# Hybrid block: one block-diagonal product inside the state chain, ScalarE evictions with scalings, output projection over two heads, a redrawn plan

## The chip, the cores and the metric

The kernel runs on one core of one Trainium2 chip. The metric is the device time of one execution in microseconds. Five instruction streams run in their own order: TensorE (PE), VectorE (DVE), ScalarE (ACT), GpSimd (POOL) and SyncE (SP), which issues the DMAs. They meet only at semaphores.

## The reference

The input x is 2 sequences of 1024 tokens with 256 features, in float32. Three layers are applied, each added to x:

1. A gated delta-rule attention with 16 heads of 128 features. From the normed input come q, k and v (projection, causal convolution over 4 tokens, silu; q and k scaled to length 1), a decay g per feature and a factor beta per token. Then per head, token by token:

```python
S = S * gt[..., None]
pred = jnp.einsum('bhk,bhkv->bhv', kt, S)
delta = (vt - pred) * bt[..., None]
S = S + kt[..., None] * delta[:, :, None, :]
o = jnp.einsum('bhk,bhkv->bhv', qt, S)
```

   o is normed, multiplied by a sigmoid gate and projected back to 256 features by Wo.
2. A gated FFN of width 1024, a state-space scan (512 channels, 16 states), and the same FFN again.

## The kernel before

**Attention phase.** The 1024 tokens are cut into 2 segments (`NSEG`) of 512, and a unit of work g is one head in one segment, for both sequences: 32 units (`NG`), called heads below. In a unit the tokens of each sequence form 8 chunks of 64 (`NC`, `CH`), and a tile of 128 partitions holds one chunk of both sequences. Inside a chunk the delta rule is a triangular system. Its inverse is built for 32-token blocks in `inverse`, from products that `products` makes in five levels, and the two 32-blocks of a chunk are then joined in `Y64`.

Before the change the system is solved ahead of the chain: `solved` multiplies the inverse with all values (U, L522) and with all keys (W, L531), for which `turn_k` turns the decayed keys (L498). ScalarE copies these results out of PSUM (L1015, L1027, L1036). The chain `state` then has two steps for each of the 8 chunks: TensorE makes pred (L567) and the state's part of the output (L572), VectorE subtracts pred (L827); TensorE makes the outer product (L577), VectorE forms the new state with the chunk's decay (L832). After every fourth chunk come the products within the chunks (L583). `output` norms, gates and turns the result, projects it with Wo (L609, four products a head), and VectorE adds each into x (L870).

**What sets the order.** Every engine's program is made by `att_drive`: each stage of each head is a generator, and `braid` runs its steps in the order of keys 100·(g+lag)+place, with lag and places from `PLACES`. One head is thus 100 units of place. The same keys rule on all five engines, so each engine has one fixed order. `EARLY_AT`, `FRONT_AT` and `FFN_AT` do the same for the first two FFN tiles and for the phase behind attention. Weights come by SyncE, one head ahead.

**Tail phase.** After a barrier (`all_over`) come the scans of 4 units, the rest of the FFN tiles, and the stores. The change touches only the places there.

## Time and profile before

| what | value |
|---|---|
| median of three runs (lowest, highest) | 2775.3 us (2770.25, 2782.81) |
| the profiled execution, its time | 2776.06 us |
| the profiled execution, its span | 2774.3 us |
| PE busy | 2495.6 us, 90% of the span, 46512 matmul records |
| DVE busy | 2124.1 us, 77% |
| ACT busy | 1393.4 us, 50% |
| POOL busy | 1260.3 us, 45% |

The span is the time from the first to the last instruction of the profiled execution; 1.8 us of its own time lie around it. One float32 product of the program appears as two matmul records, a transpose as one. Busy time counts overlapping instructions once. The attention phase takes the first 2001 us of the span, the tail the rest.

### The profile page before, as it was taken

The page shows a single profiled execution, that of the slowest core. Times are in us where ns is not written, and L with a number is a line of the kernel's source. Part 1 is how long each engine was busy: PE and PEld are TensorE (multiplying, and loading weights), DVE is VectorE, ACT ScalarE, POOL GpSimd, SP SyncE. Part 2 cuts the span into 40 slices and gives each one's busy share as a digit, 9 for nine tenths or more (in the row PEclk, how much of TensorE's full clock was granted, in tenths as well). Part 3 has the DMA queues.
Part 4 walks back from the last instruction along what each step waited for, and adds up shares of the span by engine and source line. Part 5 has one row for each costly group of instructions (what it writes and reads, how often), then busy time and mean ns, then how long its engine had stood idle before and what let it go on. Part 6 is the DMA issues. An engine that isn't in the chain of part 4 may idle for free.

```text
span 2774.3 us, 102732 instructions
## 1 busy us (share of the span) xinstructions
PE 2495.6 (90%) x46512; PEld 1483.1 (53%) x46512; DVE 2124.1 (77%) x3249; ACT 1393.4 (50%) x2647; POOL 1260.3 (45%) x989
## 2 busy tenths in 40 slices
PE   6799999999999999999999999989878889888888
PEld 3466666666666566666666666664323333333333
DVE  3778888888888787888888877863229989999981
ACT  3445555455545455455555554533255645556342
POOL 0545545555555444555555454540014645546540
PEclk9899999999999999999999999999989999999999
DMA  1000000000000000000000000010012323323320
GB/s 52 22 12 14 13 20 13 15 13 20 13 16 13 13 20 13 16 13 20 13 15 15 18 13 15 7 52 1 25 38 92 126 92 112 112 90 127 121 95 15
DMA packets 52069, 105.61 MB, mean 38 GB/s; under 512 B 7084, under 2 KB 11948, under 8 KB 51376
## 3 DMA queue, kind: packets, MB, share of 16 engines
q1 hardware_dynamic: 51632, 99.04, 11.0%
q8 instruction: 365, 5.98, 0.9%
q14 instruction: 72, 0.59, 0.1%
HBM read 96.65 MB, written 2.37 MB: 36 GB/s over the span
## 4 chain that ended last, share of the span: by engine, by line
PE 60%; DVE 15%; issue 12%; ACT 11%; POOL 1%; DMA 1%; SPq 0%; DVEq 0%; ACTq 0%; POOLq 0%
PE bank L359 8%; PE bank L461 5%; DVE hs L1683 5%; PE bank L609 4%; PE bank L424 4%; PE pair L577 3%; PE bank L1500 3%; PE pair L567 3%; PE bank L393 2%; PE bank L583 2%; PE bank L549 2%; PE bank L531 2%; PE bank L1422 2%; PE bank L572 2%; DVE cv L651 2%
## 5 line engine op out<-in xcount | busy, mean ns | idle before, releaser
L1989 POOL TENSOR_TENSOR dBu<-dtu,Bn 128x1024 f32<-128x1024 f32 x128 | 306.2, 2394 | 232.1 <-DVE hc L1690 231.8
L651 DVE SCALAR_TENSOR_TENSOR cv<-raw,taps,cv 128x1024 f32<-128x1024 f32 x288 | 385.1, 1338 | 16.4 <-ACT cv L917 14.0
L359 PE MATMUL bank<-xn,W 128*128 128x512 f32 x768 | 381.9, 621 | 0.0
L1176 POOL TENSOR_TENSOR kL<-kL,tot 128x512 f32<-128x512 f32 x128 | 195.2, 1525 | 258.0 <-PE bank L424 258.0
L916 ACT ACTIVATE raw<-bank 128x512 f32<-128x512 f32 x192 | 114.9, 599 | 370.9 <-PE bank L359 370.1
L1500 PE MATMUL bank<-hc,eye 128*128 128x512 f32 x512 | 249.1, 615 | 56.2 <-DVE hc L1690 56.1
L1887 ACT ACTIVATE bank<-dtv,m_A 128x512 f32<-128x512 f32 x256 | 174.3, 687 | 209.6 <-DVE hs L1683 208.8
L1151 POOL TENSOR_TENSOR R<-qn,gate 128x1024 f32<-128x1024 f32 x32 | 108.6, 3393 | 269.5 <-ACT gate L977 269.5
L1500 PEld LDWEIGHTS bank<-hc,eye 128*128 128x128 f32 x512 | 93.7, 193 | 201.8 <-DVE hc L1690 110.6
L359 PEld LDWEIGHTS bank<-xn,W 128*128 128x128 f32 x768 | 132.3, 191 | 112.9 <-issue 103.0
L1690 DVE TENSOR_TENSOR hc<-hs,Cn 128x1024 f32<-128x1024 f32 x128 | 171.9, 1343 | 11.5 <-PE bank L1500 7.3
L1178 POOL TENSOR_TENSOR R<-R,tot 128x512 f32<-128x512 f32 x128 | 168.4, 1316 | 0.0
L1683 DVE TENSOR_TENSOR_SCAN hs<-bank,carry,dBu 128x512 f32<-128x512 f32 x128 | 158.8, 1270 | 1.5 <-ACT bank L1887 1.5
L1683 DVE TENSOR_TENSOR_SCAN hs<-bank,dBu 128x512 f32<-128x512 f32 x128 | 150.8, 1206 | 10.1 <-POOL dBu L1989 5.0
L737 DVE TENSOR_TENSOR R<-R,tot 128x512 f32<-128x512 f32 x128 | 111.5, 871 | 47.0 <-PE bank L424 47.0
L424 PE MATMUL bank<-R,kL 128*32 128x64 f32 (+1 forms) x10240 | 135.3, 205 | 9.9 <-POOL R L1151 9.0
L577 PE MATMUL pair<-vT,kT 64*128 64x128 f32 x1024 | 129.9, 331 | 14.2 <-DVE vT L827 13.4
L424 PEld LDWEIGHTS bank<-R,kL 128*32 128x32 f32 x10240 | 115.5, 111 | 47.1 <-issue 37.3
L1073 ACT ACTIVATE cen<-bank 128x128 f32<-128x128 f32 x256 | 67.4, 278 | 145.4 <-PE bank L583 145.4
L461 PE MATMUL bank<-XY,Bc 32*32 32x32 f32 x8192 | 101.0, 195 | 42.1 <-issue 34.5
L827 DVE TENSOR_TENSOR vT<-vT,pair 128x128 f32<-128x128 f32 x256 | 71.5, 279 | 86.5 <-PE pair L567 86.2
L609 PE MATMUL bank<-WT,WO 128*128 128x512 f32 x256 | 137.1, 618 | 0.3 <-ACT WT L1090 0.3
(267 smaller groups left out, 5657.4 us busy)
## 6 DMA issues: line engine op xcount, KB each, us to landing
Bn<-ssm_rows SPq DMA_DIRECT2D x128, 256.0 KB, 3.5
Cn<-ssm_rows SPq DMA_DIRECT2D x128, 256.0 KB, 3.2
W<-in_head_w SPq DMA_DIRECT2D x32, 448.0 KB, 3.3
WO<-in_out_w SPq DMA_DIRECT2D x32, 192.0 KB, 2.3
xT<-in_xT SPq DMA_DIRECT2D x1, 2048.0 KB, 8.1
out_xT<-xT SPq DMA_DIRECT2D x4, 512.0 KB, 3.8
xn<-in_w_gate SPq DMA_DIRECT2D x1, 1024.0 KB, 5.8
xn<-in_w_up SPq DMA_DIRECT2D x1, 1024.0 KB, 8.3
```

Of the source, the lines that this page charges most:

```text
L359: m = pe.matmul(psum[bank][:, :], w[:, (kind * KT + k) * P:(kind * KT + k + 1) * P], xn[:, k, b, cols], start=k == 0, stop=k == KT - 1)
L424: m = pe.matmul(o, block(kL[s], c, b, u), r)
L461: m = pe.matmul(psum[INV][quad(w), c * SUBB:(c + 1) * SUBB], lhsT[quad(w), c, :], rhs[quad(w), c, :])
L577: m = pe.matmul(psum[CHAIN[b]][:, P:2 * P], kT[s][rows_of(b), c, :], vT[g % 3][rows_of(b), c, :])
L609: pe.matmul(psum[bank][:, :], WO[s][:, (k + 1) * P:(k + 2) * P], WT[s][:, 4 * hh:4 * hh + 4, :].rearrange("p c n -> p (c n)")).then_inc(wo ...
L651: dve.scalar_tensor_tensor(cv[m % 2][:, :, :], raw[m % 2][:, :, i:i + SEG], taps[:, h, KQV[n], i:i + 1], cv[m % 2][:, :, :], MUL, ADD).the ...
L1176: pool.tensor_tensor(Lv[:, :, 0, :], Lv[:, :, 0, :], spread(two[:, :, 1], 2, half), MUL).then_inc(up_l.sem)
L1500: m = pe.matmul(psum[Y_BANKS[jj]][:, :], eye[:, :], hc[(u * PAIRS + p) % BACK][:, jj, :], start=False, stop=p % HALF_P == HALF_P - 1, skip ...
L1683: dve.tensor_tensor_scan(hs[p % BACK][:, jj, :], psum[A_BANKS[at % NA]][:, :], dBu[p % AHEAD][:, jj, :], carry[:, b, i:i + 1] if seg else ...
L1690: dve.tensor_tensor(hc[p % BACK][:, :, :], hs[p % BACK][:, :, :], spread(Cn[p % DEEP][:, :], 1, DT2), MUL).then_inc(hc_set.sem)
L1887: act.activation(psum[A_BANKS[at % NA]][:, :], dtv[u % 2][:, j, :], ACT.Exp, scale=m_A[:, j, n:n + 1]).then_inc(dA_set.sem)
L1989: pool.tensor_tensor(dBu[at % AHEAD][:, :, :], dtu[s][:, half * DT2:(half + 1) * DT2, :], spread(Bn[at % DEEP][:, :], 1, DT2), MUL).then_i ...
```

## The change

- The chain has three steps for each chunk. pred is made from the decayed keys as they are (`R`). VectorE forms r = v·|k| − pred in one instruction. TensorE multiplies r with `Y64`, which is now a full 128 by 128 block-diagonal matrix for both sequences. ScalarE evicts the result with the scale beta/|k|² (`bs`), which gives the delta. The outer product follows as before, and VectorE only adds it, since ScalarE has scaled the old state by the chunk's decay.
- `solved`, the turning of the decayed keys, and their five kinds of evictions are gone; so are GpSimd's `side` and its making of `Y64`.
- The evictions of the turned v and the turned k and of AT's upper part move from VectorE to ScalarE, and four copies for `Y64` come onto ScalarE.
- Wo's product runs for every second head: two heads are accumulated in one PSUM bank, and VectorE adds it into x half as often.
- `qn` and `gate` have one buffer in place of two, `WO` and `bs` three in place of two; `th` and `ogT` get their own. ScalarE now waits with the gate's first eviction for the first level of the head before.
- All places are new. The columns of `PLACES` are, in order: conv 0, 1, 2, dots, gating, turn_v, products, inverse, turn_k, (solved, gone), out_gate, state, output.

```diff
@@ PLACES @@
-    (0, [-8.2, 14.4, 26.7, 27.6, 33.5, 34.5]),
...
-    (2, [7.5, 13.7, 17.5, 19.7, 23.3, 28, 31.9, 35.9, 37.3, 47.4, 50.9, 53.2, 55.5, 57.8, 67, 69.4, 72.9,
-         73.7]),
...
+    (0, [-9.7, -9.7, -3.8, 0.5, 15.2, 39.7]),
+    (0, [46.8, 46.9, 47.1, 58.2, 74.2, 106.2]),
+    (0, [-3.5, 0.5, 0.5, 54.8, 72.5, 76.3]),
+    (1, [-20.5, -10.7, -7.1, -5.5, 3.6, 5.3, 19.2, 30.6, 36.5, 41.8, 48.9, 55.6, 59.8, 65.8, 79]),
+    (1, [10, 21.7, 23.9, 31.1, 36.6, 48.2, 48.2, 53.5, 53.5, 59.3, 59.9, 62.5, 64.6, 64.7, 65.8, 71.4, 76.1,
+         83.3, 89.2, 93.2, 95.4]),
+    (1, [80.2, 82.1]),
+    (2, [18.1, 32.8]),
+    (2, [-4.3, 0.9, 6.3, 13.8, 18.9, 21.3, 24.2, 31.2, 31.3, 33.9, 36.6, 37.6, 39.9, 47.1, 48.8, 51.7, 54.9,
+         59.2, 59.4, 61.5, 63.3, 67.9, 70.5, 72.3, 75.7, 79.4]),
...
@@ hybrid_block @@
-        Y64 = sa("Y64", [P, NC, 2, SUBB])
+        Y64 = [sa(f"Y64_{i}", [P, NC, P]) for i in range(2)]
...
@@ att_tensor @@
-            def solved(g):
-                for q in range(2):
-                    bank = take()
-                    if q == 0:
-                        pe.wait_ge(*off_kept.at(g))
-                        pe.wait_ge(*vT_set.at(g, 1))
-                    for c in range(4 * q, 4 * q + 4):
-                        for b in range(NB):
-                            m = pe.matmul(psum[bank][rows_of(b), (c % 4) * P:(c % 4 + 1) * P],
-                                          Y64[rows_of(b), c, :, :].rearrange("p h i -> p (h i)"), vT[g % 3][rows_of(b), c, :])
-                    m.then_inc(u_full.sem)
-                    held[bank] = u_set.at(g, q)
-                    yield
-                w_banks = [take() for b in range(NB)]
-                pe.wait_ge(*kRT_set.at(g, 1))
-                for c in range(NC):
-                    for b in range(NB):
-                        m = pe.matmul(psum[w_banks[b]][:, c * CH:(c + 1) * CH], kRT(g)[rows_of(b), c, :],
-                                      Y64[rows_of(b), c, :, :].rearrange("p h i -> p (h i)"))
-                m.then_inc(w_full.sem)
-                for b in range(NB):
-                    held[w_banks[b]] = wT_set.at(g, b)
...
                     if c:
                         pe.wait_ge(*s_set.at(g, c - 1))
                     else:
-                        pe.wait_ge(*wT_set.at(g, 1))
+                        pe.wait_ge(*up_k.at(g, NL))
                         if g == 0:
                             pe.wait_ge(*s_zeroed.at(0))
                     for b in range(NB):
-                        m = pe.matmul(psum[CHAIN[0]][rows_of(b), 0:P], WT[s][:, c, rows_of(b)], src[:, b, :])
+                        m = pe.matmul(psum[CHAIN[0]][rows_of(b), 0:P], R[s][:, 0, c, b, :], src[:, b, :])
                     m.then_inc(pred_full.sem)
+                    yield
+                    pe.wait_ge(*r_set.at(g, c))
+                    pe.matmul(psum[CHAIN[1]][:, 0:P], Y64[s][:, c, :], vT[g % 3][:, c, :]).then_inc(solved.sem)
                     if c == 4:
                         pe.wait_ge(*og_set.at(g, 0))
+                    elif c == 0:
+                        pe.wait_ge(*up_q.at(g))
+                        if g:
+                            pe.wait_ge(*og_set.at(g - 1, 1))
                     for b in range(NB):
                         pe.matmul(psum[OUT][rows_of(b), (c % 4) * P:(c % 4 + 1) * P], R[s][:, 1, c, b, :], src[:, b, :],
                                   start=c % 4 == 0, stop=False, skip_group_check=True)
                     yield
                     pe.wait_ge(*d_set.at(g, c))
+                    if c == 0:
+                        pe.wait_ge(*kT_set.at(g, 1))
+                        if g:
+                            pe.wait_ge(*s_set.at(g - 1, NC - 1))
                     for b in range(NB):
                         m = pe.matmul(psum[CHAIN[b]][:, P:2 * P], kT[s][rows_of(b), c, :], vT[g % 3][rows_of(b), c, :])
                     m.then_inc(outer_full.sem)
                     yield
                     if c % 4 == 3:
+                        if c == 3:
+                            pe.wait_ge(*at_set.at(g))
                         for c4 in range(c - 3, c + 1):
                             for b in range(NB):
                                 m = pe.matmul(psum[OUT][rows_of(b), (c4 % 4) * P:(c4 % 4 + 1) * P],
...
                 for hh in range(2):
                     for k in range(KT):
-                        bank = take()
-                        if k == 0:
-                            pe.wait_ge(*ogT_set.at(g, hh))
-                        pe.matmul(psum[bank][:, :], WO[s][:, (k + 1) * P:(k + 2) * P],
-                                  WT[s][:, 4 * hh:4 * hh + 4, :].rearrange("p c n -> p (c n)")).then_inc(wo_full.sem)
-                        held[bank] = x_added.at(g, 2 * hh + k)
+                        if g % 2:
+                            bank = take()
+                            if k == 0:
+                                pe.wait_ge(*ogT_set.at(g, hh))
+                                if hh == 0:
+                                    pe.wait_ge(*wo_scaled.at(g))
+                            for i in range(2):
+                                m = pe.matmul(psum[bank][:, :], WO[(g - 1 + i) % 3][:, (k + 1) * P:(k + 2) * P],
+                                              ogT[i][:, 4 * hh:4 * hh + 4, :].rearrange("p c n -> p (c n)"),
+                                              start=i == 0, stop=i == 1)
+                            m.then_inc(wo_full.sem)
+                            held[bank] = x_added.at(g // 2, 2 * hh + k)
                         if 2 * hh + k < 3:
...
@@ att_vector @@
-                dve.wait_ge(*at_diag.at(g))
-                for w in (0, 2):
-                    m = dve.tensor_tensor(AT[s][quad(w), :, SUBB:CH], view[quad(w), :, 1, :],
-                                          spread(bs[s][quad(w), :], 2, SUBB), MUL)
-                m.then_inc(at_set.sem)
...
                 for c in range(NC):
-                    src = S[:, h, :, :] if c % 2 == 0 else Sx[:, :, :]
                     dst = Sx[:, :, :] if c % 2 == 0 else S[:, h, :, :]
                     dve.wait_ge(*pred_full.at(g, c))
                     if c == 0:
-                        dve.wait_ge(*u_set.at(g, 1))
-                    dve.tensor_tensor(vT[g % 3][:, c, :], vT[g % 3][:, c, :], psum[CHAIN[0]][:, 0:P],
-                                      SUB).then_inc(d_set.sem)
-                    yield
+                        dve.wait_ge(*vT_set.at(g, 1))
+                        dve.wait_ge(*k_norm.at(g))
+                        dve.wait_ge(*off_kept.at(g))
+                    dve.scalar_tensor_tensor(vT[g % 3][:, c, :], vT[g % 3][:, c, :], knorm[g % 3][:, c:c + 1],
+                                             psum[CHAIN[0]][:, 0:P], MUL, SUB).then_inc(r_set.sem)
+                    yield
+                    yield
+                    dve.wait_ge(*s_scaled.at(g, c))
                     dve.wait_ge(*outer_full.at(g, c))
-                    for b in range(NB):
-                        m = dve.scalar_tensor_tensor(dst[:, b, :], src[:, b, :], tot_chunk[s][:, c, b:b + 1],
-                                                     outer[:, b, :], MUL, ADD)
-                    m.then_inc(s_set.sem)
+                    dve.tensor_tensor(dst[:, :, :], dst[:, :, :], outer, ADD).then_inc(s_set.sem)
                     yield
                     if c == 3:
...
@@ att_scalar @@
-                    if b == 0 and g >= 2:
-                        act.wait_ge(*w_full.at(g - 2))
-                    act.activation(by_batch(gate[s])[:, b, :, :], psum[bank][:, :].rearrange("p (c t) -> p c t", t=CH),
+                    if b == 0 and g:
+                        act.wait_ge(*level.at(g - 1, 1))
+                    act.activation(by_batch(gate)[:, b, :, :], psum[bank][:, :].rearrange("p (c t) -> p c t", t=CH),
...
+                for half in range(2):
+                    bank = turn.next()
+                    act.wait_ge(*v_turned.at(g, half))
+                    if g >= 3:
+                        act.wait_ge(*within_full.at(g - 3, 1))
+                    act.activation(vT[g % 3][:, 4 * half:4 * half + 4, :].rearrange("p c d -> p (c d)"), psum[bank][:, :],
+                                   ACT.Copy).then_inc(vT_set.sem)
+                    if half == 0:
+                        yield
...
+                act.wait_ge(*bo_set.at(g))
+                act.wait_ge(*at_diag.at(g))
+                for w in (0, 2):
+                    m = act.activation(AT[g % 2][quad(w), :, SUBB:CH],
+                                       psum[PROD][quad(w), :].rearrange("p (c a i) -> p c a i", c=NC, a=2)[:, :, 1, :],
+                                       ACT.Copy)
+                m.then_inc(at_set.sem)
...
+                act.wait_ge(*y_set.at(g, NL - 1))
+                if g >= 2:
+                    act.wait_ge(*solved.at(g - 2, NC - 1))
+                else:
+                    act.wait_ge(*y64_zeroed.at(g))
+                for w in range(4):
+                    m = act.activation(Y64[g % 2][quad(w), :, quad(w)], XY[quad(w), 1, :, :], ACT.Copy)
+                m.then_inc(y64_set.sem)
...
+                    act.wait_ge(*k_turned.at(g, q))
+                    if g >= 2:
+                        act.wait_ge(*outer_full.at(g - 2, NC - 1))
+                    act.activation(kT[s][:, 4 * q:4 * q + 4, :].rearrange("p c d -> p (c d)"), psum[bank][:, :],
+                                   ACT.Copy).then_inc(kT_set.sem)
+                    if q == 0:
...
+                h, s = g % H, g % 2
+                for c in range(NC):
+                    src = S[:, h, :, :] if c % 2 == 0 else Sx[:, :, :]
+                    dst = Sx[:, :, :] if c % 2 == 0 else S[:, h, :, :]
+                    if c:
+                        act.wait_ge(*s_set.at(g, c - 1))
+                    else:
+                        act.wait_ge(*up_t.at(g, NL - 1))
+                        act.wait_ge(*(s_set.at(g - 1, NC - 1) if g else s_zeroed.at(0)))
+                    for b in range(NB):
+                        m = act.activation(dst[:, b, :], src[:, b, :], ACT.Copy, scale=tot_chunk[s][:, c, b:b + 1])
+                    m.then_inc(s_scaled.sem)
+                    yield
+                    if c == 0:
+                        act.wait_ge(*bs_set.at(g))
+                    act.wait_ge(*solved.at(g, c))
+                    act.activation(vT[g % 3][:, c, :], psum[CHAIN[1]][:, 0:P], ACT.Copy,
+                                   scale=bs[g % 3][:, c:c + 1]).then_inc(d_set.sem)
+                    yield
+                    yield
+                    if c == 3:
+                        yield
 
...
```

## Rows read from the trace of the kernel before

**Rows 1.** Busy time by stretch: columns are stretch, length, PE, PEld, DVE, ACT, POOL, granted clock, DMA.

```profile
1142.00:1579.00 437.00, 412.75 (x11169) 280.01 (x11168) 364.43 (x664) 240.91 (x504) 234.57 (x192) 1.00 0.05 16
229.96:288.40 58.44, 53.99 (x1398) 36.84 (x1400) 46.34 (x84) 30.30 (x64) 29.05 (x28) 0.94 0.05 14
171.00:1695.00 1524.00, 1429.79 (x37712) 968.24 (x37712) 1244.95 (x2243) 816.97 (x1706) 778.93 (x688) 0.98 0.05 15
1695.00:2001.00 306.00, 279.68 (x4880) 171.99 (x4878) 168.30 (x317) 123.91 (x256) 85.16 (x73) 0.96 0.05 16
2101.00:2693.00 592.00, 518.51 (x1142) 212.06 (x1140) 554.14 (x491) 309.58 (x480) 314.93 (x146) 0.98 0.34 110
```

**Rows 2.** Waits of PE from 1142 to 1579 us: total us, times, longest.

```profile
PE bank L461 <- issue: 12.4, 13, 1.4
PE bank L449 <- issue: 5.2, 4, 1.5
PE pair L577 <- DVE vT L827: 1.6, 2, 0.8
```

**Rows 3.** Groups by form on PE, 1142 to 1579 us: count | busy us, mean ns | idle before.

```profile
L609 PE MATMUL bank<-WT,WO 128*128 128x512 f32 x64 | 34.4, 619 | 0.0
L549 PE MATMUL bank<-WO,hga 128*128 128x128 f32 x128 | 18.8, 289 | 0.2 <-issue 0.2
L522 PE MATMUL bank<-vT,Y 64*64 64x128 f32 x256 | 17.5, 275 | 0.5
L531 PE MATMUL bank<-Y,gate 64*128 64x64 f32 x256 | 16.0, 275 | 0.0
L567 PE MATMUL pair<-S,WT 128*64 128x128 f32 x128 | 14.1, 297 | 0.7 <-issue 0.6
L498 PE MATMUL bank<-eye,R 128*128 128x128 f32 x64 | 10.0, 279 | 0.0
```

**Rows 4.** Groups by form on VectorE, 1142 to 1579 us.

```profile
L651 DVE SCALAR_TENSOR_TENSOR cv<-raw,taps,cv 128x1024 f32<-128x1024 f32 x72 | 94.3, 1309 | 0.6
L870 DVE TENSOR_TENSOR xT<-xT,bank 128x512 f32<-128x512 f32 x32 | 21.9, 684 | 9.4 <-PE bank L609 9.4
L832 DVE SCALAR_TENSOR_TENSOR Sx<-S,tot_chunk,pair 128x128 f32<-128x128 f32 x64 | 18.9, 336 | 0.0
L827 DVE TENSOR_TENSOR vT<-vT,pair 128x128 f32<-128x128 f32 x64 | 17.9, 280 | 13.5 <-PE pair L567 13.4
L747 DVE TENSOR_TENSOR Bc<-bank,bm 128x256 f32<-128x256 f32 x40 | 16.5, 413 | 0.0
L699 DVE TENSOR_TENSOR vT<-bank,knorm 128x512 f32<-128x512 f32 x16 | 11.0, 686 | 5.3 <-PE bank L405 5.3
```

**Rows 5.** Groups by form on ScalarE, 1142 to 1579 us.

```profile
L917 ACT ACTIVATE cv<-bank,taps 128x512 f32<-128x512 f32 x48 | 32.8, 683 | 0.0
L1073 ACT ACTIVATE cen<-bank 128x128 f32<-128x128 f32 x64 | 16.9, 278 | 26.2 <-PE bank L583 26.2
L1053 ACT ACT_TABLE_LOAD x8 | 10.3, 1283 | 0.1
L1036 ACT ACTIVATE WT<-bank 128x512 f32<-128x512 f32 x16 | 8.7, 595 | 17.6 <-PE bank L531 17.6
L1001 ACT ACTIVATE Z<-bank 32x256 f32<-32x256 f32 x16 | 6.0, 378 | 0.3
L1056 ACT ACTIVATE WO<-WO,norm_w 128x256 f32<-128x256 f32 x8 | 4.0, 497 | 0.0
```

**Rows 6.** Timeline: start us, us, instruction [idle before]; one chunk's steps, at two places.

```profile
1254.84 0.44 PE L567 MATMUL pair<-Sx,WT 128*64 128x128 f32 x4
...
1255.33 0.29 DVE L827 TENSOR_TENSOR vT<-vT,pair 128x128 f32<-128x128 f32 x1 [0.50 <-PE pair L567]
...
1844.15 0.28 DVE L827 TENSOR_TENSOR vT<-vT,pair 128x128 f32<-128x128 f32 x1
...
1844.49 0.49 PE L577 MATMUL pair<-vT,kT 64*128 64x128 f32 x4 [0.39 <-DVE vT L827]
```

251 lines of the change are left out of this document (91 added, 160 removed), and 12 rows, old and new, of tables (EARLY_AT, PLACES).

## The prediction, made before the run

> **What bounds the kernel now.** I read the busy time by stretch first. From 1142 to 1579 us eight heads pass, at full clock: 437.0 / 8 = 54.6 us a head, of which TensorE is busy 412.75 / 8 = 51.6 us, VectorE 45.6, ScalarE 30.1, GpSimd 29.3 [rows 1]. So TensorE idles 3.0 us a head. The waits say what for: nearly all of it is "issue" in front of streams of tiny products (12.4 and 5.2 us in eight heads at L461 and L449), where no engine is waited for; the chain (L577 behind L827) costs 1.6 us in eight heads, 0.2 a head [rows 2]. The attention phase is therefore bound by TensorE's own work, and the order written into the places hides every other engine. The granted clock adds to it: over 27 heads from 171 to 1695 us it is 0.98, and a head takes 1524 / 27 = 56.4 us; in one head at 0.94 it is 58.4 us [rows 1]. The tail is another matter: from 2101 to 2693 us VectorE is busy 554 of 592 us [rows 1], and the change alters only places there.
>
> **TensorE's work.** Removed in each head: U, 17.5 / 8 = 2.19 us; W, 16.0 / 8 = 2.00; the turning of the decayed keys, 10.0 / 8 = 1.25 [rows 3]. Together 5.44 us. Added: eight products of 128 by 128 with 128 columns, 16 records. The nearest row is the gate product L549, of just this shape: 18.8 / 128 = 0.147 us a record, so 16 × 0.147 = 2.35 us [rows 3]. Bounds: the narrower L567 has 14.1 / 128 = 0.110, so 1.76 us; a product that stands alone shows its first record's 289 ns and then 0.147, so 8 × 0.436 = 3.5 us. I take 2.35, since other products stand around most of them. pred from `R` has the shape of the pred from WT, so its cost stays. Wo's product keeps its count: four products a head before, eight for every second head after, so nothing is saved on TensorE. Net 5.44 − 2.35 = −3.1 us a head. Records fall from 1396 to 1396 − 72 + 16 = 1340 a head (11169 / 8, rows 1), and the issue stalls, which stand before streams of tiny products, I let fall by the same 4%: −0.1 us.
>
> **VectorE's work.** Gone: two evictions of the turned v at 0.686 [rows 4], two of the turned k of the same size, two of AT's upper part (a bank read of 256 columns, as L747, 0.41), and two of the four additions into x at 0.684: 1.37 + 1.37 + 0.82 + 1.37 = 4.9 us. In the chain a chunk had 0.280 + 2 × 0.336 = 0.95 us [rows 4]; now it has one three-operand instruction of 128 columns, priced as L832, 0.336, and one addition of 256 columns, as L747, 0.413: 0.75, so −1.6 us in eight chunks. VectorE goes from 45.6 to about 39 us. It is not the bound, so this is worth nothing by itself; it makes the answers in the chain earlier.
>
> **ScalarE's work.** Removed: six evictions of 512 columns at about 0.60 = −3.6 us. Added: four of these for turned v and k, 2.4; AT and the four copies into `Y64`, 6 × 0.378 = 2.3 (L1001) [rows 5]; eight evictions of the solved chunk, 128 columns from PSUM as L1073, 0.278, with a scale vector, which from L1036 to L917 costs 0.683 − 0.595 = 0.09: 8 × 0.37 = 2.9; sixteen scalings of the state, 128 columns within SBUF. L1056 has 256 columns with a scale in 0.497; by L1073 and L1001 a column costs (378 − 278) / 128 = 0.8 ns, so 0.39 us each, 6.3 us (bounds 0.28 and 0.50 each: 4.5 and 8.0). Sum +10.3 us: ScalarE goes to some 40 us, 77% of a head of 52. Its cover is that TensorE still has more; it becomes a server that every chunk needs, in a fixed order with other work.
>
> A rule of the Trainium skill speaks against this move: "ScalarE: Activation LUTs", Rules for kernel authors, says to do plain multiplications and additions on VectorE and budgets about 0.3 us and 0.83 ns an element for each ScalarE instruction, 0.41 us for 128 columns. By it the 24 new small instructions take 9.8 us, where my terms say 9.2; the trace agrees with its slope and shows less fixed cost, and the sum stays. What it would mean if ScalarE came to be waited for is the slower rival.
>
> **GpSimd and SyncE.** GpSimd loses the side product and `Y64`; it has half its time free, so zero. SyncE's loads only change the buffer they go to; the third `WO` buffer lets Wo stay until the second head of a pair has used it. Zero.
>
> **The chain.** Each chunk has three round trips where it had two. From row to row: pred starts at 1254.84 and VectorE at 1255.33, 0.49 later; VectorE ends at 1844.43 and TensorE starts at 1844.49, 0.06 later [rows 6]. Between pred and the solving product lie 0.49 + 0.34 + 0.06 = 0.89 us; between that and the outer product about 0.29 + 0.05 + 0.37 + 0.06 = 0.77; from there to the next pred 0.49 + 0.05 + 0.41 + 0.06 = 1.0. TensorE must have other work for it. I merged the new places as `braid` does and priced what stands between. After pred: 0.55 us or more in every chunk (an inverse step of 0.69, the dots, the gate product), with pred's own 0.3 just enough. After the outer product: 0.55 to 1.1 us beside its own 0.42, enough within 0.1. After the solving product: itself and the state's part of the output, 0.29 + 0.32 = 0.61, and a block of 0.69 or so in chunks 0, 1, 4, 5 and 6; in chunks 2, 3 and 7 nothing, 0.15 us short each. That makes 0.6 us a head if VectorE and ScalarE are free when asked. They are not always: a convolution step holds VectorE 1.31 us [rows 4], a table load ScalarE 1.28 [rows 5]. The second half of the new chain (places 47 to 76) has no projection beside it; about 14 us of VectorE's work stand against 13 of TensorE's there. I add 0.6 for this, 1.2 against 0.2 now, so +0.9 to 1.0 us a head. Behind a waiting product stands all of TensorE's order, so each such wait counts in full. Low end: 0; high end in the rival.
>
> **Single buffers.** The gate's first eviction now waits for level one of the head before, whose VectorE part is some 4 us after the first level's products. ScalarE stands in that wait, with the chain's first delta behind it. In the merged order the projections are ahead of it; I count it within the 1.2.
>
> **The sum.** A head: 54.6 − 3.1 − 0.1 + 0.9 = 52.3 us, −2.3 us. I apply it to 32 heads, the last ones included (from 1695 to 2001 us TensorE is still busy 280 of 306 us, rows 1): −74 us. When the last head runs out, its longer chain has only the early FFN beside it: +2. The tail's new places: 0, between −8 and +8, as VectorE leaves only 38 us of 592 unused there [rows 1]. The profiled execution, 2776.06 us, becomes 2704; it stands 0.8 above the median of the runs, so 2703.
>
> **Rivals.**
> (a) *The order hides everything.* Waits stay at 0.2: −3.2 us a head, −102: about 2674. For it: today's order hides two round trips almost wholly. Against: three chunks have no block between solving and outer product.
> (b) *A third round trip that is half covered.* 2.4 us of waits a head: −1.0 × 32 = −32: about 2743. For it: the stretch without projections and ScalarE at 77%.
> (c) *ScalarE's order sets the pace; slower than before.* The eight deltas queue on ScalarE behind silus, exps and table loads of about 1.1 to 1.3 us, three loads a head [rows 5]. It decides from 3.2 + 0.2 = 3.4 us of waits a head, 0.43 a chunk. If each chunk lost 0.8 us, 6.4 a head: +6.2 − 3.2 = +3.0 × 32 = +96: about 2871; at 0.5 a chunk 2794. Against: ScalarE has 12 us a head free, and its copies of Z, also in a chain, cost TensorE nothing today [rows 2].
> (d) *The clock.* If all heads ran at 54.6's clock, 27 × 1.8 = 49 us would be won; if all ran as the one at 0.94, 27 × 2.0 = 54 lost [rows 1]. Nothing in the change pushes it clearly; it widens the range.
> (e) *No gain, since what is removed was cover.* U, W and the turns give the other engines 5 us a head to catch up, and without them the waits grow by as much: about 2775. Against: three of these blocks lie at the seam between heads, where TensorE waits for nobody.
>
> **Chances.** Forecast (2680 to 2725) 0.50; (a) 0.13; (b), to 2761, 0.21; (e) 0.05; (c) 0.11. About 0.5%, 14 us, is what a measurement of this kernel can tell from no change: faster 0.84, same 0.05, slower 0.11. The range 2657 to 2766 takes in (a) with some luck of the clock, and (b).
>
> **What would show it.** In the changed profile, in a stretch at full clock: a head of 52 to 52.5 us; TensorE busy 48.5; the new product at 0.15 us a record; ScalarE near 40 us busy, VectorE 39; new lines in TensorE's waits, 1 us a head for VectorE's r and ScalarE's delta, most of it at chunks 2, 3 and 7. It is wrong if TensorE's waits for ScalarE pass 2 us a head (b, c), if the clock in the heads leaves 0.96 to 1.0, or if the tail moves by more than 8 us.

## The result and the profile after

| | before | after |
|---|---|---|
| median of four runs each (lowest, highest) | 2775.69 us (2770.25, 2782.81) | 2854.74 us (2848.57, 2860.58) |
| ratio, 95% interval | | 1.0283 (1.025 to 1.0316) |
| span of the profiled execution | 2774.3 us | 2855.4 us |

The change makes the kernel 2.8% slower; 2703 us had been forecast, and 2766 was the end of the range. The two spans differ by 81.1 us. SyncE's loads of `W` mark the heads: from the sixth to the last lie 26 heads in both kernels. They took 1464.97 us before and 1540.82 after, +76. What comes ahead of them is 9 us shorter, from the last load to the attention's end there are 337 us in place of 306 [rows 1], +31, and the tail is 16 us shorter.

Busy time by stretch, columns as in [rows 1]. First the 26 heads of the kernel before:

```profile
229.96:1694.93 1464.97, 1375.67 (x36314) 931.31 (x36316) 1198.47 (x2160) 786.70 (x1643) 749.89 (x661) 0.98 0.05 15
```

The kernel after: its 26 heads, an odd head at full clock, one at 0.92, an even head, the end of the attention.

```profile
220.60:1761.42 1540.82, 1387.57 (x34858) 922.62 (x34860) 1164.47 (x1743) 1079.87 (x2422) 682.46 (x610) 0.94 0.05 14
570.56:629.45 58.89, 54.03 (x1350) 34.96 (x1352) 45.01 (x70) 41.31 (x93) 26.08 (x25) 1.00 0.05 14
1287.89:1351.17 63.28, 57.37 (x1350) 37.57 (x1352) 47.42 (x70) 41.63 (x93) 26.05 (x22) 0.92 0.04 13
1351.17:1405.61 54.44, 47.48 (x1334) 31.84 (x1336) 44.72 (x65) 41.43 (x93) 26.40 (x22) 1.00 0.05 15
1761.42:2098.00 336.58, 296.78 (x5032) 175.39 (x5032) 167.81 (x267) 175.78 (x392) 83.89 (x69) 0.93 0.04 15
```

Per head (divide by 26): the period goes from 56.35 to 59.26 us. TensorE is busy 53.37 us where it was 52.91, and idle 5.89 where it was 3.43. The clock is 0.94 against 0.98. ScalarE is at 41.5 us (forecast 40), VectorE at 44.8 (forecast 39), GpSimd at 26.2.

Waits of TensorE in the 26 heads after (as [rows 2]):

```profile
PE bank L458 <- issue: 54.5, 44, 2.3
PE bank L372 <- issue: 33.9, 26, 2.5
PE bank L458 <- ACT Z L969: 23.2, 24, 1.0
PE pair L531 <- DVE Sx L791: 13.7, 13, 1.3
PE bank L420 <- DVE Ac L696: 6.4, 23, 0.3
PE pair L535 <- DVE vT L785: 4.1, 6, 0.7
PE pair L552 <- ACT vT L1047: 3.2, 6, 0.6
```

The reader is to see which rows are short: the two that the new round trip brought, `L535` for VectorE's r and `L552` for ScalarE's delta, have 7.3 us in 26 heads, 0.3 a head. What grew is "issue", from 2.8 to 3.5 us a head (the largest row before is the one below), and waits that the prediction did not have at all: 0.9 us a head for ScalarE's `Z` and 0.5 for the state.

```profile
PE bank L461 <- issue: 47.7, 38, 2.7
```

The solving product on TensorE after, 163 to 1761 us (27 heads; as [rows 3]):

```profile
L535 PE MATMUL pair<-vT,Y 128*128 128x128 f32 x432 | 106.3, 330 | 6.8 <-DVE vT L785 4.1 <-issue 2.7
```

The solving product takes 106.3 / 27 = 3.9 us a head by its own rows at the clock of the run, 0.25 a record, where 0.147 had been taken.

**Where the clock goes.** TensorE, kernel after, at the start of an odd head: products, the table load that stands ahead of `Z` on ScalarE, then the same time by stretches of 5 us.

```profile
1172.15 0.67 PE L458 MATMUL bank<-Z,XY 32*32 32x32 f32 x54
1174.20 0.31 PE L458 MATMUL bank<-Z,XY 32*32 32x32 f32 x10 [1.38 <-issue]
...
1178.04 0.44 PE L372 MATMUL bank<-qn 128*32 128x32 f32 x15 [1.48 <-issue]
1178.41 0.80 PE L535 MATMUL pair<-vT,Y 128*128 128x128 f32 x2
...
1188.94 0.75 PE L458 MATMUL bank<-Z,XY 32*32 32x32 f32 x64 [0.96 <-ACT Z L969]
...
1185.90 1.28 ACT L900 ACT_TABLE_LOAD   x1
```

```profile
1170.00:1175.00 5.00, 3.62 (x191) 2.80 (x184) 2.73 (x5) 4.95 (x9) 2.61 (x2) 0.98 0.27 95
1175.00:1180.00 5.00, 3.52 (x150) 2.82 (x148) 2.80 (x6) 3.31 (x5) 1.07 (x1) 0.50 0.03 7
1180.00:1185.00 5.00, 5.00 (x169) 4.15 (x160) 1.79 (x4) 1.08 (x3) 1.49 (x2) 0.50 0.02 5
1185.00:1190.00 5.00, 4.03 (x153) 2.98 (x148) 4.16 (x8) 4.35 (x11) 0.76 (x2) 1.00 0.01 3
```

Two stalls of 1.4 us stand 2.4 us apart in a long run of tiny products. In the stretch with the first of them TensorE is busy 3.62 of 5 us, and by its end the clock falls from full (2.4 GHz) to half (1.2 GHz), for about 10 us. A solving product then takes 0.80 us where it takes 0.49. The even head from 1351 us has stalls of 1.45 and 1.33 us, 2.1 us apart, and keeps the full clock:

```profile
1356.00:1361.00 5.00, 2.61 (x168) 2.13 (x167) 2.50 (x4) 4.05 (x6) 1.45 (x2) 1.00 0.01 3
```

So the clock falls behind such stalls in some places and not in others; what decides it is not shown. The Trainium skill, "TensorE: Matmul & The Clock Gate", section "HAM oscillation — how this bites in real kernels", tells of longer gaps, waits for transfers between bursts of products: the clock falls in the gap and the next burst starts slow. The slow products behind the stalls of the odd head agree; the even head has no such fall.

**VectorE and GpSimd on one port.** Timeline of the kernel after:

```profile
1371.62 3.35 DVE L691 TENSOR_TENSOR R<-kL,gate 128x1024 f32<-128x1024 f32 x1
...
1371.52 2.36 POOL L1145 TENSOR_TENSOR R<-qn,gate 128x1024 f32<-128x1024 f32 x1 [6.67 <-PE bank L560]
```

The same pair in the kernel before:

```profile
1267.73 1.23 DVE L713 TENSOR_TENSOR R<-kL,gate 128x1024 f32<-128x1024 f32 x1 [1.38 <-ACT gate L977]
...
1267.78 3.40 POOL L1151 TENSOR_TENSOR R<-qn,gate 128x1024 f32<-128x1024 f32 x1 [7.82 <-ACT gate L977]
```

VectorE's instruction is called rk below. Both multiply two tensors in SBUF. The one that starts first, by 0.05 or 0.10 us, takes its own time, and the other takes that and its own: 1.2 + 2.2 = 3.4, 2.3 + 1.1 = 3.4. The order has turned round: before, GpSimd, which has time, paid; after, VectorE pays. The Trainium skill, "SBUF — State Buffer", section "Who interferes with whom", states that a VectorE instruction with two inputs in SBUF contends with a GpSimd instruction that reads SBUF, and that the order of issue decides who blocks. The rows agree.

The same happens to an instruction of 8 columns, `osum`, which took 0.16 us in the kernel before (L852) and now starts while GpSimd makes its masks:

```profile
1375.49 2.14 DVE L809 SCALAR_TENSOR_TENSOR osum<-norms,osum 128x8 f32<-128x8 f32 x1
...
1373.85 3.75 POOL L1151 TENSOR_TENSOR bm<-masks,bs 128x1536 f32<-128x1536 f32 x1
```

It ends when they are done, and its mean over the 26 heads is 2.02 us. In the whole run ScalarE waits 50 us for it. This was not tested by a run.

### The profile page after: what moved, and what is told of

The parts are those of the page before. It is cut to its first block, busy times and chain, and to the rows that moved or that the text cites. A ratio compares the mean times of both kernels' runs of the same rounds, so it can differ in the third digit from the quotient of the medians.

```text
span 2855.4 us, 100153 instructions
## 1 busy us (share of the span) xinstructions
PE 2512.6 (88%) x44720; PEld 1470.2 (51%) x44720; DVE 2071.2 (73%) x2737; ACT 1759.9 (62%) x3610; POOL 1184.8 (41%) x927
## 4 chain that ended last, share of the span: by engine, by line
PE 59%; DVE 16%; issue 13%; ACT 11%; DMA 1%; POOL 0%; DVEq 0%; SPq 0%; ACTq 0%; POOLq 0%
PE bank L354 7%; PE bank L458 6%; DVE hs L1663 5%; PE bank L590 4%; PE pair L552 4%; PE bank L1480 3%; PE pair L535 3%; PE bank L420 3%; PE pair L531 3%; PE bank L513 3%; PE bank L1402 2%; PE bank L543 2%; PE bank L372 2%; PE bank L446 2%; ACT vT L1047 1%
## 5 line engine op out<-in xcount | busy, mean ns | idle before, releaser
L634 DVE SCALAR_TENSOR_TENSOR cv<-raw,taps,cv 128x1024 f32<-128x1024 f32 x288 | 393.0, 1365 | 35.3 <-ACT cv L875 34.6
L1166 POOL TENSOR_TENSOR kL<-kL,tot 128x512 f32<-128x512 f32 x128 | 211.6, 1653 | 426.6 <-PE bank L420 425.9
L354 PE MATMUL bank<-xn,W 128*128 128x512 f32 x768 | 360.7, 610 | 0.0
L1480 PE MATMUL bank<-hc,eye 128*128 128x512 f32 x512 | 254.6, 626 | 47.6 <-DVE hc L1670 47.5
L354 PEld LDWEIGHTS bank<-xn,W 128*128 128x128 f32 x768 | 141.0, 193 | 151.8 <-issue 147.9
L1047 ACT ACTIVATE vT<-pair,bs 128x128 f32<-128x128 f32 x256 | 93.9, 367 | 161.4 <-PE pair L535 161.3
L458 PE MATMUL bank<-Z,XY 32*32 32x32 f32 x8192 | 109.7, 200 | 74.7 <-issue 46.1
L785 DVE SCALAR_TENSOR_TENSOR vT<-vT,knorm,pair 128x128 f32<-128x128 f32 x256 | 86.5, 338 | 111.8 <-PE pair L531 99.2
L1145 POOL TENSOR_TENSOR R<-qn,gate 128x1024 f32<-128x1024 f32 x32 | 78.2, 2444 | 208.2 <-PE bank L560 196.0
L715 DVE TENSOR_TENSOR R<-R,tot 128x512 f32<-128x512 f32 x128 | 123.4, 964 | 52.2 <-PE bank L420 52.2
L552 PE MATMUL pair<-vT,kT 64*128 64x128 f32 x1024 | 135.4, 343 | 14.5 <-ACT vT L1047 5.1
L458 PEld LDWEIGHTS bank<-Z,XY 32*32 32x32 f32 x8192 | 91.0, 111 | 106.7 <-issue 60.0
```

The costliest lines, as they stand in the source:

```text
L354: m = pe.matmul(psum[bank][:, :], w[:, (kind * KT + k) * P:(kind * KT + k + 1) * P], xn[:, k, b, cols], start=k == 0, stop=k == KT - 1)
L458: m = pe.matmul(psum[INV][quad(w), c * SUBB:(c + 1) * SUBB], lhsT[quad(w), c, :], rhs[quad(w), c, :])
L552: m = pe.matmul(psum[CHAIN[b]][:, P:2 * P], kT[s][rows_of(b), c, :], vT[g % 3][rows_of(b), c, :])
L634: dve.scalar_tensor_tensor(cv[m % 2][:, :, :], raw[m % 2][:, :, i:i + SEG], taps[:, h, KQV[n], i:i + 1], cv[m % 2][:, :, :], MUL, ADD).the ...
L1166: pool.tensor_tensor(Lv[:, :, 0, :], Lv[:, :, 0, :], spread(two[:, :, 1], 2, half), MUL).then_inc(up_l.sem)
L1480: m = pe.matmul(psum[Y_BANKS[jj]][:, :], eye[:, :], hc[(u * PAIRS + p) % BACK][:, jj, :], start=False, stop=p % HALF_P == HALF_P - 1, skip ...
```

## The experiments

"Waits", "period" and "idle" are those of the same 26 heads. Each group of runs shared its runs of the kernel before; the ratio is to those.

**The tail alone.** The kernel before with the four lists of places of the tail from the change:

```
-FFN_FROM = [0, 0, 52.3, 142.6, 242.7, 342.7, 430.8, 531.5]
+FFN_FROM = [0, 0, 52.3, 142.5, 242.6, 334.2, 426.8, 526.6]
...
```

> The kernel before with only the places of the tail phase (scans and late FFN) taken from the change. The tail took 773 us before (2001 to 2774) and 757 in the changed kernel (2098 to 2855). Theory: the redrawn tail places are worth this by themselves: about -16 us, 2760 us, the attention phase unchanged at 2001 us. Rival: the shorter tail is what the longer attention phase left behind or chance, and here it is within 5 us of before.

Measured: 2759.65 us (2754.39 to 2764.14), ratio 0.9946 (0.9929 to 0.9963). The tail's new places give 15 us by themselves, and this is the fastest kernel here that computes the whole: it beats both.

**One more product in each chunk, or eight in a row.** In the kernel before:

```
                     m.then_inc(pred_full.sem)
+                    pe.matmul(psum[CHAIN[1]][:, 0:P], eye[:, :], eye[:, :])
```

> The kernel before with one more 128x128x128 product in each chunk of the chain (identity by identity, into an unused part of a bank, never read), put between pred and the state's part of the output; no wait is added. Theory A (a short product that stands alone between others of another shape costs TensorE 0.42 us and makes its neighbours dearer by 0.1 to 0.15, as L535 in the changed kernel shows): +4.0 to 4.6 us a head, +130 to +145 us, about 2910. Rival (the price of my prediction, 0.29 us each, 2.35 us a head): +75 us, 2850.

```
+                        for c in range(NC):
+                            pe.matmul(psum[CHAIN[1]][:, 0:P], eye[:, :], eye[:, :])
                     for c in range(4 * hh, 4 * hh + 4):
```

> The same eight extra products a head, but in a row in front of the gate products, which have the same shape. Both theories: 0.147 us a record, 2.35 us a head, +75 us, 2850. By theory A this is 50 to 70 us faster than the run with them inside the chain; by the rival the two are equal within 10 us.

Measured: 2860.4 us, ratio 1.0302 (1.0272 to 1.0332), for the scattered ones: +85.6 us, 2.68 a head over all 32, 0.33 a product. In a row: 2827.28, ratio 1.0189 (1.0156 to 1.0221): +52 us, 1.64 a head, 0.205 a product. The 26 heads of the two runs:

```profile
230.85:1770.28 1539.43, 1485.76 (x36730) 987.51 (x36732) 1188.68 (x2159) 783.79 (x1643) 714.78 (x660) 0.98 0.05 14
232.20:1750.35 1518.15, 1427.36 (x36730) 981.16 (x36732) 1203.85 (x2160) 786.55 (x1643) 740.44 (x661) 0.98 0.05 15
```

By these periods a product costs 0.36 us scattered and 0.26 in a row. So a product of this shape alone between others costs 1.4 to 1.6 times what it costs in a row. The first expectation was too high by 50 us. In a row the added 2.0 us of busy time lengthen the period by all of it, 2.05; the scattered ones add 4.2 us of busy time and 2.9 to the period, since they take up 1.4 us of what had been waits. The mean clock is 0.98 in both runs, as in the kernel before.

**Places set by hand.** The changed kernel with the shared stages at their places of before and places that I set for the chain:

> The changed kernel with other places for the heads: those of the kernel before for all stages it shares, and the chain's 26 steps set by hand so that a block of other work stands between nearly all of them. Theory B (the redrawn order leaves TensorE waiting; 2.4 us a head more idle time than before): idle falls by 2 us a head, about 2790 us. Rival (the third round trip and ScalarE's load make the waits in any order, and the clock falls with them): within 15 us of the changed kernel, 2840 to 2870.

Measured: 3201.15 us, ratio 1.1533 (1.1496 to 1.157). TensorE waited 89 us for `cen`, 85 for the delta, 69 for r. Nothing follows on the change, but much on the order: places alone moved this kernel by 346 us.

**The gating behind k's step.**

```
-    (0, [56.8, 59.4, 65.1, 74.8]),
-    (0, [-3.5, 0.5, 0.5, 54.8, 72.5, 76.3]),
+    (0, [56.8, 59.4, 66.2, 74.8]),
+    (0, [-3.5, 0.5, 0.5, 66.5, 72.5, 76.3]),
```

> The changed kernel with two places redrawn: the gating step (exp, ln) is put behind the dots' step in the order, so that both exps and the ln of a head stand together and the silu of k goes before them. Table loads fall from 5 to 3 a head. Theory (the loads are one of the uncounted costs: 2.6 us of ScalarE a head, in front of Z, for which TensorE waits 0.9 us a head at L458): that wait falls to under 0.3 and the head by 0.8 to 1.0 us, 30 us in all, about 2825. Rival (the loads lie in ScalarE's free time, and Z is late for other reasons): less than 5 us, and within 2850 to 2858.

Measured: 2954.7 us, ratio 1.0637 (1.0619 to 1.0655). The loads fell to three, and the wait for `Z` went from the list. But its longest wait is now

```profile
PE pair L552 <- ACT vT L1047: 103.5, 32, 3.6
```

once in each head. ScalarE and TensorE there:

```profile
1440.59 1.04 ACT L932 ACTIVATE sq<-sq 128x1024 f32<-128x1024 f32 x1
1441.66 1.15 ACT L934 ACTIVATE sq<-sq,biases 128x1024 f32<-128x1024 f32 x1
1442.72 0.58 ACT L946 ACTIVATE vT<-bank 128x512 f32<-128x512 f32 x1
1443.19 0.68 ACT L1041 ACTIVATE S<-Sx,tot_chunk 128x128 f32<-128x128 f32 x2
1443.78 0.35 ACT L1047 ACTIVATE vT<-pair,bs 128x128 f32<-128x128 f32 x1
...
1439.81 0.49 PE L535 MATMUL pair<-vT,Y 128*128 128x128 f32 x2
...
1444.18 0.80 PE L552 MATMUL pair<-vT,kT 64*128 64x128 f32 x4 [3.52 <-ACT vT L1047]
```

The solved chunk was ready at 1440.3, and three small steps behind a table load and four long ones stood ahead of its delta. My repair removed two table loads a head, 2.6 us of ScalarE's work, and put a wait of 3.2 us into every head: this is rival (c), made by hand. It also means that the price of the two extra loads was not measured.

**GpSimd behind rk.**

```
-                pool.wait_ge(*gate_set.at(g))
+                pool.wait_ge(*rk_set.at(g))
```

> The changed kernel, in which GpSimd's gating of q waits until VectorE has made rk; nothing else is altered. Theory (VectorE and GpSimd hold each other up where both read SBUF, and the new order lets GpSimd's 2.4 us instruction start first): VectorE's rk falls from about 3.3 us back to 1.2, VectorE's steps behind it come 2 us earlier in each head, and the head loses 0.3 to 0.8 us: 2830 to 2845. Rival (VectorE has time there, and what waits is not its work): rk gets short, the time stays within 5 us of the changed kernel's.

Measured: 2829.77 us (2825.24 to 2835.48), ratio 1.0189 (1.0169 to 1.0209): 25 us less than the change. VectorE, kernel after, 1160 to 1706 us:

```profile
L691 DVE TENSOR_TENSOR R<-kL,gate 128x1024 f32<-128x1024 f32 x9 | 27.4, 3041 | 0.0
...
L706 DVE TENSOR_TENSOR tot<-gate 128x512 f32<-128x512 f32 x9 | 16.7, 1854 | 0.0
```

and in this run:

```profile
L691 DVE TENSOR_TENSOR R<-kL,gate 128x1024 f32<-128x1024 f32 x9 | 10.6, 1182 | 0.0
...
L706 DVE TENSOR_TENSOR tot<-gate 128x512 f32<-128x512 f32 x9 | 6.1, 681 | 0.0
```

These two rows give back 1.86 + 1.17 = 3.0 us of VectorE a head in these heads. Over the 26 heads all of VectorE's busy time falls by 0.86 a head only, since other instructions now lie beside GpSimd's (`cen`, L815, goes from 1.2 to 2.3 us, and `osum` stays at 1.8). The period falls by 0.56 us, and TensorE's wait for `Ac`, 6.4 us, is gone. The port is a cost of the change, shown; one wait moved it and did not remove it.

**Without the solving product.** The inverse is left out, and ScalarE scales r where it lies:

```
-                    pe.wait_ge(*r_set.at(g, c))
-                    pe.matmul(psum[CHAIN[1]][:, 0:P], Y64[s][:, c, :], vT[g % 3][:, c, :]).then_inc(solved.sem)
```

> The changed kernel without the eight solving products of a head: ScalarE scales r itself in its place, so the chain has two trips through TensorE and one through each of the two others, and the output is not the reference's. Theory A (the product and its round trip cost more than the whole predicted gain: 3.75 us of TensorE plus most of the new waits for r and delta): 4.5 us a head less, 2700 to 2725. Rival (the product costs its records alone, and the added waits come from the order around it, from table loads and from GpSimd): 2.3 to 2.9 us a head, 2760 to 2780.

Measured: 2758.05 us, ratio 0.993 (0.9915 to 0.9945): 97 us less than the change, 3.0 a head, between the two expectations and a little nearer to the rival.

```profile
213.66:1683.21 1469.55, 1303.93 (x34442) 853.35 (x34444) 1163.58 (x1743) 1079.12 (x2422) 694.69 (x610) 0.95 0.05 15
```

TensorE's busy time falls by (1387.57 - 1303.93) / 26 = 3.2 us a head; idle is 6.4 where it was 5.9. So the product costs its work, 3.2 and not 2.35, and no waits of its own; the period falls by 2.7. And here is the surprise: U, W, the turns and this product are all gone, by [rows 3] 5.4 us a head of the kernel before, by TensorE's busy time 2.8, and the time equals that of the kernel before with the new tail (2759.65).

**The state's decay on VectorE.** As before, on the path behind the outer product:

```
-                    dve.tensor_tensor(dst[:, :, :], dst[:, :, :], outer, ADD).then_inc(s_set.sem)
+                    for b in range(NB):
+                        m = dve.scalar_tensor_tensor(dst[:, b, :], src[:, b, :], tot_chunk[s][:, c, b:b + 1],
+                                                     outer[:, b, :], MUL, ADD)
```

> The changed kernel with the state's decay done as before: two three-operand instructions on VectorE after the outer product, no scaling on ScalarE. It takes 16 instructions of about 0.39 us off ScalarE a head, and adds about 0.26 us a chunk to VectorE on the chain. Theory (ScalarE's load, 41.5 us a head, makes Z, vT and the deltas late): 15 to 30 us faster, 2825 to 2840. Rival (ScalarE is not what is waited for, and the scaling takes work off the chain): same or up to 15 us slower, 2855 to 2870.

Measured: 2855.91 us, ratio 1.0282 (1.0261 to 1.0304): no difference, the rival. ScalarE falls from 41.5 to 36.9 us a head for nothing.

**v's projection among the tiny products, alone and with the port's repair.**

```
-    (0, [46.8, 46.9, 47.1, 58.2, 74.2, 106.2]),
+    (0, [57.5, 62, 62.2, 66, 74.2, 106.2]),
```

> The changed kernel with v's places redrawn: the two halves of its projection stand at 57.5 and 62 in place of 46.8 and 46.9, the convolution steps behind them at 62.2 and 66. So 3.7 us of products with 512 columns lie in the middle of the 20 us in which TensorE now gets only tiny products. Theory (tiny products without long ones between them run TensorE out of instructions, two stalls of about 1.4 us come close together, and after them the clock falls to half for some 9 us in every second head): a head loses 1.5 to 3 us and the granted clock rises to 0.96 or more: 2770 to 2810. Rival (the stalls belong to the number of instructions, wherever the long products stand, and the clock has another reason): within 10 us of the changed kernel, 2845 to 2865.

> Both repairs in one: v's projection between the tiny products, and GpSimd's gating of q behind VectorE's rk. Theory (they are separate costs and add): 25 us below the run with v's projection alone, 2745 to 2785. Rival (both fill the same wait for Z at the end of the tiny products): less than 10 us below it.

Measured: 2981.17 us, ratio 1.0758 (1.0726 to 1.0789), and 2981.93, ratio 1.0756. Waits of the first:

```profile
PE pair L535 <- DVE vT L785: 81.3, 26, 3.2
PE pair L531 <- DVE Sx L791: 48.9, 38, 1.9
PE bank L458 <- DVE XY L754: 39.4, 26, 1.5
PE bank L372 <- issue: 11.3, 17, 1.6
PE bank L458 <- issue: 10.8, 13, 1.1
```

"Issue" fell from 88 to 22 us, as the theory had it. But the convolution's steps moved with the projection, and VectorE's r is now late once a head, by 3.1 us: 170 us of waits for VectorE in these three rows, in place of 14 + 4, and the clock at 0.89. These waits may themselves have taken the place of stalls; the run does not separate the two. With these waits the port's repair is worth nothing.

**The early FFN's places as before.**

> The changed kernel with the places of the two early FFN parts as before; all else stays. Theory (the drain is 31 us longer because the longer chain has too little beside it, whatever these places are): within 8 us of the changed kernel. Rival (the redrawn early places cost the drain): 15 to 30 us faster, 2825 to 2840.

Measured: 2857.7 us, ratio 1.0308 (1.0284 to 1.0333): within 3 us of the change, and from the last load of `W` to the end of the span 1099 us pass, in the change 1094. The 31 us at the end of the attention are not from these places.

**Wo over two heads in the kernel before, with the new tail.**

```
-                        pe.matmul(psum[bank][:, :], WO[s][:, (k + 1) * P:(k + 2) * P],
+                            for i, t in enumerate((ogT, WT[1])):
+                                m = pe.matmul(psum[bank][:, :], WO[(g - 1 + i) % 3][:, (k + 1) * P:(k + 2) * P],
+                                              t[:, 4 * hh:4 * hh + 4, :].rearrange("p c n -> p (c n)"),
+                                              start=i == 0, stop=i == 1)
```

> The kernel before with two parts of the change alone: the tail's places, and Wo's product accumulated over two heads (three buffers of WO, o's transpose of the even head in a buffer of its own); solving, scalings and all places of the attention stay. The tail's places alone gave 2760. Theory (the part saves what its records show, 4.3 - 3.75 = 0.5 us of TensorE and two additions of VectorE a head, and no wait takes its place): 12 to 18 us less, 2742 to 2748. Rival (the order was drawn for even heads that also had this product; the instruction stalls grow by as much): 2755 to 2765.

Measured: 2797.91 us, ratio 1.0095 (1.0067 to 1.0123): 38 us slower than the tail alone. TensorE's busy time is the same, 1375.55 against 1376.70 us in 26 heads, so the saving of 0.5 us that I had read from group sums does not exist. The even heads lose four products, and there

```profile
PE pair L578 <- DVE vT L834: 32.8, 32, 1.6
PE pair L568 <- DVE S L839: 11.4, 13, 0.9
```

where the tail alone has 12.9 for `vT` and nothing for `S`.

**U and W left out in the order of before** (12 of 16 and 14 of 16 products of a head are missing):

```
-                    for c in range(4 * q, 4 * q + 4):
+                    for c in range(4 * q + 3, 4 * q + 4):
...
-                for c in range(NC):
+                for c in range(NC - 1, NC):
```

> The kernel before, in its own order, with 12 of U's 16 products and 14 of W's 16 left out in each head (all evictions and steps stay; the output is not the reference's). Their records are 24 of 32 and 28 of 32: 2.19 x 0.75 + 2.00 x 0.875 = 3.4 us of TensorE a head. Theory (removed work was cover, and comes back as waits for the other engines and as instruction stalls): less than half of it is won, 0 to 55 us, 2720 to 2775. Rival (the order hides the other engines with room to spare, as the prediction had it): 3.0 to 3.4 us a head, 2665 to 2680.

Measured: 2775.0 us, ratio 0.9984 (0.9964 to 1.0003). Nothing is won.

```profile
228.38:1692.07 1463.69, 1306.87 (x34962) 856.46 (x34964) 1217.38 (x2160) 784.81 (x1643) 742.81 (x661) 0.98 0.05 15
```

```profile
PE bank L424 <- POOL R L1151: 28.5, 26, 1.1
PE pair L577 <- DVE vT L827: 21.0, 47, 0.8
PE bank L522 <- ACT cv L917: 18.2, 26, 0.7
...
PE bank L600 <- ACT WT L1090: 10.3, 26, 0.4
```

TensorE's busy time falls by 2.65 us a head and its idle time grows by 2.60. The waits are for all three other engines, and three of the four have no row in the waits of the kernel before; "issue" stays at 2.8 us a head. This run decides the case: TensorE was busy 94% of the period, and yet less of its work does not shorten it. More of it does lengthen it, as the eight products in a row showed. So TensorE and some loop through the other engines stood level. The longest of the new waits, 1.1 us a head, is for GpSimd's gating of q, which takes 3.4 us there because VectorE holds the port first, and 2.4 by itself. Whether that port sets the old period was not tested.

**Filling the gaps.** The changed kernel:

```
+                    if c in (4, 5):
+                        for _ in range(6):
+                            pe.matmul(psum[CHAIN[1]][:, 0:P], eye[:, :], eye[:, :])
                     pe.wait_ge(*r_set.at(g, c))
```

> The changed kernel with six more products of the identity by itself (128 by 128, 128 columns, 12 records) ahead of the solving product of chunks 4 and 5, next to the two instruction stalls: 24 records a head, at 0.102 a record in a row 2.5 us a head by the earlier run of eight in a row in the kernel before (1.64 / 16 records). Theory (the clock falls where TensorE has gaps, and the products fill them): the clock of the heads rises from 0.94 to 0.97 or more, and the time stays within 25 us of the changed kernel's, up or down. Rival (the clock has another reason): 60 to 100 us slower, 2915 to 2955, at a clock of 0.94.

Measured: 2880.12 us, ratio 1.0356 (1.0338 to 1.0375): +25.4 us by the medians, 20 by the ratios, at the edge of what the theory allowed.

```profile
223.59:1785.72 1562.13, 1429.83 (x35482) 971.98 (x35484) 1166.76 (x1742) 1082.92 (x2422) 682.77 (x610) 0.97 0.05 14
```

The clock rises from 0.94 to 0.97. 12 products more, 3.1 us a head by the period of the run in a row, lengthen the period by 0.82: a faster clock and 0.8 us less idle time pay for the rest. So TensorE's gaps weigh on the clock. Their sum alone does not set it: without most of U and W the kernel before is idle 6.0 us a head at 0.98, the changed kernel 5.9 at 0.94.

**Wo in every head again, alone and with the port's repair.** In the changed kernel, with the early FFN's places of before:

```
-                            for i in range(2):
-                                m = pe.matmul(psum[bank][:, :], WO[(g - 1 + i) % 3][:, (k + 1) * P:(k + 2) * P],
+                        pe.matmul(psum[bank][:, :], WO[g % 3][:, (k + 1) * P:(k + 2) * P],
```

> The changed kernel with Wo's product in every head again, four products and four additions a head (and the early FFN places of before, worth 3 us by a run of their own). By its records 0.5 us a head more of TensorE and two additions more of VectorE. Theory (the product of 512 columns is cover for the chain in even heads, as the kernel before showed when it lost it, 38 us): 0 to 30 us faster, 2825 to 2855. Rival (in the changed order even heads are the short ones, 54.5 us against 63.3, so there is nothing to cover): 15 to 40 us slower, 2870 to 2895.

> The run before this one with GpSimd's gating of q behind VectorE's rk besides. Theory (separate costs): 25 us below it. Rival (with more of VectorE's additions in even heads the order of the two engines shifts): within 8 us of it.

Measured: 2864.37 us, ratio 1.0298 (1.0279 to 1.0317), and 2837.96, ratio 1.021 (1.0193 to 1.0227). The first falls between both expectations: the wait for the state goes (13.7 to 3.0 us), one for `ogT` comes (8.5) and the stalls grow. In the order of before the same product was worth 38 us, here nothing. The second is 26 us below the first, as the repair gave 25 alone; beside v's moved projection it gave nothing.

## Why the prediction was wrong

The miss is 153 us of span: 136 in the 26 heads (forecast -60, came +76), 33 at both ends of the attention (forecast -12, came +21), and -16 in the tail. In a head it is 5.2 us: 2.2 of TensorE's work, 1.7 of waits, 1.3 of the clock.

- **The step that failed** is the first: "the attention phase is therefore bound by TensorE's own work, and the order written into the places hides every other engine". It was read from short waits. They show that the others are not late; they don't show by how much they are early. With most of U and W gone from an unchanged order, 3.4 us by their rows and 2.65 of busy time, all of it came back as waits for ScalarE, VectorE and GpSimd, and the time stayed (ratio 0.9984). Rival (e) named this and got 0.05, with the argument that three of the removed blocks lie at the seam between heads; U at that seam waits for ScalarE's `cv` in the run without them. In the changed order TensorE's work counts: 3.2 us less of it gave 2.7. Which loop between the engines sets the 56.3 us was not found. Nor is it shown how much of the 2.9 us a head by which the change is slower belongs to its chain and how much to its new places: no run has the one without the other, but for the places set by hand.
- **TensorE's work**, forecast -3.1 us a head. At full clock it is busy 47.5 in an even head and 54.0 in an odd one (one head of each), 50.7 on average, against 51.6: -0.85. The solving product costs 3.2 in place of 2.35; the lower rate came from the gate products, which stand in a row, and the upper bound, 3.5, was right beside it and was dismissed because other products stand around it. That is the very case in which a lone product is dear, 1.4 to 1.6 times one in a row. Most of the rest is pred and output, no longer back to back: 0.37 + 0.37 us from start to start, before 0.27 + 0.32, 1.2 us a head, not counted. Wo's term, zero, was right.
- **The waits**, forecast +0.8 in sum, came +2.5. Those reckoned in detail, for r and delta, are 0.3 us a head, less than forecast. The others were not on the list: `Z`, ahead of which ScalarE now loads a table for k's exp and ln (five loads a head for three, since the gating's exp and ln come before k's; what the loads cost was not measured), the state, VectorE held up by GpSimd, and 0.7 us more of "issue", where the forecast had 0.1 less. "GpSimd: zero" was wrong: its load fell, its moment moved. One wait against it gave 25 us back.
- **The loads of the other engines.** VectorE was to fall from 45.6 to 39 us a head and is at 44.8. The steps of the chain cost what was forecast; `rk`, 3.05 us for 1.23, and `osum`, 2.02 for 0.16, alone add 3.7, both beside GpSimd. ScalarE's 41.5 comes near the forecast 40 by luck: it holds 2.6 us of table loads that were not in it.
- **The clock**, held open as (d), took 1.3 us a head. It was treated as weather; but six products in the gaps of two chunks brought it from 0.94 to 0.97, so gaps in TensorE's work can cost twice, as time and as clock. Which gaps do is not shown.
- **The ends**: the last heads were to gain and the drain to cost 2; the last stretch is 31 us longer, with the clock at 0.93. In the last chunks 3.9 us pass from one solving product to the next, at half clock, with nothing beside them. The early places are not the cause; how the rest divides is open.
- **The tail**: 0 forecast, -15 measured by itself. Places alone could do that, though VectorE is busy 554 of 592 us [rows 1].
- **Rival (c)** had the sign and, by its 2794 to 2871, the time, but not the way: taking 4.6 us a head off ScalarE changed nothing. A single badly placed block on ScalarE does what (c) describes.

## What to carry to other kernels

Where the order of work is fixed, a busy engine with short waits may stand level with the others: before crediting removed work, leave it out in the old order and time that. Price an added small product by one that stands alone, and a moved GpSimd instruction by whom it meets on the shared port, not by its load. Ask of a gap on TensorE also what it does to the clock behind it: stalls of about the same length left it full in one head and came before its fall in another.

## What the runs showed of the hardware

- TensorE's clock fell to half for about 10 us behind a stall of 1.38 us in one head and stayed full behind stalls of 1.45 and 1.33 us in another. Products of the identity in the gaps brought the mean of the heads from 0.94 to 0.97.
- A 128 by 128 float32 product with 128 columns costs 0.205 us in a row of eight and 0.33 us alone between other shapes (time over all heads; 0.26 and 0.36 by the period of 26).
- A start 0.05 to 0.10 us earlier decides whether VectorE or GpSimd takes 3.4 us in place of 1.2 or 2.4. A VectorE instruction of 8 columns that takes 0.16 us took 2.14 beside a long one of GpSimd.
- With projections between the tiny products TensorE's "issue" stalls fell from 88 to 22 us in 26 heads, while its waits for VectorE grew by some 150.
